# Second recurrence of a two-layer block: rows of C by DMA instead of a TensorE spread and a ScalarE copy, and two banks for the rows of B

## What is computed

```python
def step(state, inp):                       # 256 channels, 16 states
    dt_t, u_t, b_t, c_t, g_t = inp
    a = a_base[None] * (0.5 + g_t)[..., None]
    decay = jnp.exp(dt_t[..., None] * a)
    state = decay * state + dt_t[..., None] * b_t[:, None, :] * u_t[..., None]
    y_t = jnp.sum(state * c_t[:, None, :], axis=-1) + D_param * u_t
    return (state, y_t)
```

## Time and profile before

| | us |
|---|---|
| median of three runs | 652.9 |
| lowest, highest | 650.82, 654.76 |
| span of the profiled execution | 652.0 |
| busy in it: TensorE, VectorE, ScalarE, GpSimd | 565.3, 529.9, 391.0, 394.1 |
| recurrence of layer 1, first to last scan | 266.7 to 494.2 |

### The profile page before, as it was taken

How to read it: one execution, slowest core, us unless ns; L and a number is a source line. 1 busy time by engine, 2 the same in 40 slices (tenths; PEclk the granted TensorE clock), 3 DMA queues, 4 the chain that set the end, 5 groups by cost and what they waited for, 6 DMA issues and landing times.

```text
span 652.0 us, 6791 instructions
## 1 busy us (share of the span) xinstructions
PE 565.3 (87%) x1896; PEld 318.0 (49%) x1896; DVE 529.9 (81%) x729; ACT 391.0 (60%) x670; POOL 394.1 (60%) x345
## 2 busy tenths in 40 slices
PE   6698668899999877898887869768789999999997
PEld 3233222376778522333332323323345778888885
DVE  1979997656779678899999999999998857666674
ACT  5675333687123498878867655766664575555553
POOL 0035896661000202499999999999875547566665
PEclk9898877999799998799999898999989999999999
DMA  8100000800210001000000000001003333434430
GB/s 309 39 2 1 0 1 1 343 1 1 66 66 1 1 0 48 2 0 1 2 24 25 25 25 25 24 14 50 0 0 115 98 114 125 127 106 147 110 102 18
DMA packets 14598, 35.13 MB, mean 54 GB/s; under 512 B 1952, under 2 KB 2240, under 8 KB 13952
## 3 DMA queue, kind: packets, MB, share of 16 engines
q1 hardware_dynamic: 14560, 34.69, 16.6%
HBM read 33.48 MB, written 1.20 MB: 53 GB/s over the span
## 4 chain that ended last, share of the span: by engine, by line
PE 33%; DVE 29%; issue 15%; POOL 13%; ACT 9%; DMA 1%; POOLq 0%; DVEq 0%; SPq 0%; ACTq 0%
DVE arena L1932 12%; POOL h_parts L2147 9%; PE ps L1081 7%; DVE arena L1907 5%; PE ps L1016 3%; PE ps L687 3%; DVE arena L1660 3%; POOL arena L2012 3%; PE ps L866 2%; DVE ps L1644 2%; DVE ps L1853 1%; PE ps L883 1%; PE ps L944 1%; PE ps L801 1%; PE ps L804 1%
## 5 line engine op out<-in xcount | busy, mean ns | idle before, releaser
L2012 POOL TENSOR_TENSOR arena<-arena 128x512 f32<-128x512 f32 x184 | 226.4, 1265 | 22.8 <-DVE arena L1932 16.8
L1932 DVE TENSOR_TENSOR_SCAN arena<-ps,carry,arena 128x512 f32<-128x512 f32 x128 | 156.8, 1268 | 0.0
L1016 PE MATMUL ps<-arena,core 128*128 128x512 f32 x256 | 128.2, 623 | 0.9 <-POOL arena L2012 0.7
L1487 ACT ACTIVATE ps<-arena,abase 128x512 f32<-128x512 f32 x128 | 88.0, 692 | 63.6 <-DVE arena L1932 62.8
L2147 POOL TENSOR_TENSOR h_parts<-arena,h_parts 128x512 fp32r<-128x512 f32 x68 | 87.7, 1290 | 63.3 <-ACT h_parts L1527 62.3
L1081 PE MATMUL ps<-x_parts,w_hi 128*128 128x512 f32 x272 | 100.4, 408 | 0.4 <-DVE arena L2005 0.4
L1907 DVE TENSOR_TENSOR arena<-ps,arena 128x1024 f32<-128x1024 f32 x64 | 77.1, 1205 | 4.6 <-PE ps L1119 4.5
L2000 DVE TENSOR_TENSOR ps<-ps,arena 128x512 f32<-128x512 f32 x64 | 44.6, 697 | 44.1 <-PE ps L1081 35.9
L1119 PE MATMUL ps<-bc,sel 96*128 96x512 bf16 x128 | 44.5, 394 | 37.9 <-ACT arena L1476 23.4
L1535 ACT ACTIVATE arena<-ps 128x512 f32<-128x512 f32 x68 | 40.6, 598 | 61.2 <-PE ps L1081 60.1
L1016 PEld LDWEIGHTS ps<-arena,core 128*128 128x128 f32 x256 | 50.2, 198 | 41.6 <-issue 26.0
(11 more groups left out here) (258 smaller groups left out, 1002.9 us busy)
## 6 DMA issues: line engine op xcount, KB each, us to landing
arena<-weight_rows SPq DMA_DIRECT2D x64, 256.0 KB, 3.3
arena<-in_wB SPq DMA_DIRECT2D x2, 2048.0 KB, 12.5
arena<-in_wD SPq DMA_DIRECT2D x8, 384.0 KB, 3.2
arena<-in_cstB SPq DMA_DIRECT2D x1, 1368.0 KB, 5.9
wC<-in_wC SPq DMA_DIRECT2D x1, 1056.0 KB, 11.8
x<-in_x SPq DMA_DIRECT2D x4, 256.0 KB, 4.8
arena<-slot_rows SPq DMA_DIRECT2D x4, 256.0 KB, 3.7
arena<-scale_rows SPq DMA_DIRECT2D x4, 256.0 KB, 3.6
```

What stands on the lines that cost most here:

```text
L1016: mm(bank(c + 2 * (i % 2)), CORE_("eye"), PRC[:, (2 * q + c) % PR_RING, :], start=False, stop=(n == NS - 1)).then_inc(*done(f"y{n}_{c}", i))
L1487: A(bank(6 + c), ch(DTG[:, c, :], i), ACT.Exp, scale=ABASE[:, c * NS + n:c * NS + n + 1]).then_inc(*done(f"dec{n}_{c}", i))
L1932: nc.vector.tensor_tensor_scan(ST[:, k % ST_RING, :], bank(6 + c), DBU[:, (2 * q + c) % DBU_RING, :], CARRY[:, k:k + 1], ALU.mult, ALU.add ...
L2012: mul = lambda o, a, b: nc.gpsimd.tensor_tensor(o, a, b, ALU.mult)
```

## The change

The rows of C no longer pass TensorE, bank 5 and ScalarE. `bc_hi` is made with a scale that is 1 for rows of B and 0 for rows of C (a new column `b_rows` of the constants), so R1 holds the rows of C whole, in f32. SP stores these 16 rows of a chunk in DRAM, and loads one row per turn over all partitions into the same ring `CBR`. GpSimd waits for the load instead of the copy. Bank 5 becomes a second bank for the rows of B. The raw expert weights, from the third part on, are issued among the rows of C at set turns (`RAW_AT`). The selection matrix loses its half for C, and a constant that nothing used (`EYEB`) goes.

```diff
+RAW_AT = {24 + 4 * k: k + 2 for k in range(WD_PARTS - 2)}
...
-            act += [(f"c_copy{n}", i)] + decs if q else decs + [("c_copy0", 0)]
+            act += decs
...
-            pe += [(f"b{n}", i), (f"c{n}", i)]
+            pe.append((f"b{n}", i))
...
+            def keep_c_rows(i):
+
+                sp.wait_ge(*upto("bc_r1", i))
+                sp.dma_start(c_rows[i * NS:(i + 1) * NS, :], ch(R1, i)[NS:2 * NS]).then_inc(c_rows_kept, 16)
+
+            def c_row(q):
+
+                i = q // NS
+                if q % NS == 0:
+                    sp.wait_ge(c_rows_kept, 16 * (i + 1))
+                if q >= C_RING:
+                    sp.wait_ge(*turn("sc{}_1", q - C_RING))
+                sp.dma_start(CBR[:, q % C_RING, :], c_rows[q:q + 1, :].partition_broadcast(P)).then_inc(c_loaded[q % C_RING], 16)
...
+            keep_c_rows(0)
+            for q in range(C_RING):
+                c_row(q)
+            for i in range(1, NCH):
+                keep_c_rows(i)
+            sp.wait_ge(*upto(f"conv1_{KC - 2}", NCH - 1))
+            raw_weights(0)
+            raw_weights(1)
+            for q in range(C_RING, NQ):
+                c_row(q)
+                if q in RAW_AT:
+                    raw_weights(RAW_AT[q])
...
-                if m == 0:
-                    pe.wait_ge(*upto(f"dbu{NS - 1}", NCH - 1))
-                elif m == 1:
-                    pe.wait_ge(*upto(f"c_copy{NS - 1}", NCH - 1))
+                if m < 2:
+                    pe.wait_ge(*turn("dbu{}", NQ - 2 + m))
...
-                for kind, b, last_use, row in ("b", 4, "dbu{}", n), ("c", 5, "c_copy{}", NS + n):
-                    if q:
-                        pe.wait_ge(*turn(last_use, q - 1))
-                    mm(bank(b), sel[:, row, :], BC[:, i * N:(i + 1) * N], start=True, stop=True).then_inc(*done(f"{kind}{n}", i))
+                if q >= 2:
+                    pe.wait_ge(*turn("dbu{}", q - 2))
+                mm(bank(4 + q % 2), sel[:, n, :], BC[:, i * N:(i + 1) * N], start=True, stop=True).then_inc(*done(f"b{n}", i))
...
-                A(ch(BC, i), half(1, i, BC3), ACT.Copy).then_inc(*done("bc_hi", i))
+                A(ch(BC, i), half(1, i, BC3), ACT.Copy, scale=col("b_rows")[0:BC3]).then_inc(*done("bc_hi", i))
...
-            nc.vector.tensor_copy(ch(BC, LAST), half(1, LAST, BC3)).then_inc(*done("bc_hi", LAST))
+            ts(ch(BC, LAST), half(1, LAST, BC3), col("b_rows")[0:BC3], None, ALU.mult).then_inc(*done("bc_hi", LAST))
...
-                    pool.wait_ge(*upto(f"c_copy{n}", i))
+                    pool.wait_ge(c_loaded[q % C_RING], 16 * (q // C_RING + 1))
```

More of the change, by code:

```diff
@@ L104 @@
 VEC = ["ln1_w", "mu_r", "mu_k", "mu_v", "mu_w", "mu_g", "w0", "u", "gn_w", "gn_b", "ln2_w",
-       "c0", "c1", "eps5", "eps6", "two", "one", "x_low", "x_sign", "w_low", "w_sign",
+       "c0", "c1", "b_rows", "eps5", "eps6", "two", "one", "x_low", "x_sign", "w_low", "w_sign",
        "dt_b0", "dt_b1", "D0", "D1", "cb0", "cb1"] + [f"cw{c}_{j}" for c in range(DI) for j in range(KC)] + \
@@ L364, with build @@
 G_LAST = ["g_half"]
[L367 removed]
+def build(nc, X_in, vec_in, core_in, cst_in, wA_in, wmod_in, cstB_in, wB1_in, wB2_in, wC_in, sel_in, wD_in, out):
     f32 = mybir.dt.float32
@@ L399, in build @@
         slots_loaded, scales_loaded = ([sem(f"{name}_loaded{i}") for i in range(NCH)] for name in ("slots", "scales"))
+        c_rows = nc.dram_tensor("c_rows", (NQ, N), f32, kind="Internal").ap()
+        c_rows_kept = sem("c_rows_kept")
+        c_loaded = [sem(f"c_loaded{k}") for k in range(C_RING)]
         row_loaded = [sem(f"row_loaded{k}") for k in range(W_SLOTS)]
@@ L645, in _, with raw_weights @@
                     sp.dma_start(ch(dst, i), token_rows[k][i:i + 1, :].partition_broadcast(P)).then_inc(landed[i], 16)
-            sp.wait_ge(*upto(f"conv1_{KC - 2}", NCH - 1))
-            for k in range(WD_PARTS):
+            def keep_c_rows(i):
[8 more added lines that the diff above has]
+                sp.dma_start(CBR[:, q % C_RING, :], c_rows[q:q + 1, :].partition_broadcast(P)).then_inc(c_loaded[q % C_RING], 16)
+            def raw_weights(k):
                 if k >= 2:
@@ L1470, in decays @@
                 i, n = divmod(q, NS)
-                def c_copy():
-                    act.wait_ge(*upto(f"c{n}", i))
-                    if q >= C_RING:
-                        act.wait_ge(*turn("sc{}_1", q - C_RING))
-                    A(CBR[:, q % C_RING, :], bank(5), ACT.Copy).then_inc(*done(f"c_copy{n}", i))
-                if q:
-                    c_copy()
-                else:
+                if q == 0:
                     act.wait_ge(*upto("sp_1", LAST))
```

24 lines of the change are left out of this document (10 added, 14 removed).

## The result

| | before | after |
|---|---|---|
| median of 20 runs each, us | 653.92 | 651.43 |
| lowest, highest | 650.82, 655.05 | 650.31, 653.31 |
| span of the profiled execution | 652.0 | 649.8 |

The ratio of the two kernels is 0.9974, with a 95% interval of 0.9962 to 0.9985 (the medians alone give 0.9962, the means 0.9972). The change gains 0.26% here, half of what the prediction called measurable, where 0.6% was forecast. The same kernel was run twice more beside the experiments, and stood there at 0.9988 and 0.9992, with intervals that take in 1. By the three ratios the gain is 0.5 to 1.7 us, not 4.

What follows compares the result with a forecast made beforehand. VectorE was taken as the bound, 3.49 us a turn. Span 652.0 - 4.7 at the seam (gaps -2.07, start +0.1 included) + 0.7 for the clock = 648.0; the median, 0.9 above the span, made it 648.9 us, range 646.3 to 650.3.

Steps and rivals of the forecast that it cites:

- (1): TensorE in the recurrence: 64 matmuls spreading C go, 25 us of TensorE beside VectorE's turns, not on the path.
- (2): ScalarE in the recurrence: 64 copies out of bank 5 go, 37.3 us, by itself worth nothing; TensorE's wait goes.
- (3): Recurrence: a second bank gives rows of B a turn more, removing VectorE's gaps of 0.31, 0.96 and 0.80: -2.07 us.
- (4): Start of the recurrence: the 2.41 us gap stays nearly whole, scaled copies cost more; net +0.1 us, bounds -0.2 and +0.4.
- (5): Seam from recurrence to experts: second up product starts at 492.2, not 496.9, so -4.7 us, containing the 2.07.
- 0.7 for the clock: Seam: a low TensorE clock takes back 0.7 us of the gain, bounds nothing and 2.6 us.
- (6): SP's queue: four stores and 64 loads for rows of C, 3.3 us each, hidden by GpSimd's work: cost nothing.
- (7): GpSimd in the recurrence: little slack, 0.3 us left at turn 35; DMA slowdown taken as 0, up to +1.1 us.
- the 2.6 of the clock: Seam: upper bound of what a low TensorE clock takes back, all the seam gives beyond the gaps.
- the first: Rival at the seam: TensorE stays at the low clock, only the gaps are gained; gain 2, 650.9 us, chance 0.18.
- Slower: Rival in the recurrence: TensorE at the low clock for many turns becomes the bound; +8, 656.9 us, chance 0.13.

Runs made afterwards that it cites:

- Experiment 1: Changed kernel with TensorE issuing the row of B of turn q+1 ahead of the y sum of turn q-4: 649.5 us, 0.9939 of the kernel before.
- experiment 3: Changed kernel with a single bank for the rows of B instead of two: 1.0009 and, second time, 0.9989 of the kernel before.
- experiment 8: Changed kernel with GpSimd's nine w_lo splits replaced by plain copies on ScalarE: 651.48 us, 0.9967 of the kernel before.
- experiment 9: Changed kernel with a TensorE wait for ScalarE's decay put back behind each row of B: median 652.59 us, 1.0017 of the kernel before.
- experiment 6: Changed kernel without the 60 loads of rows of C from turn 4 on: 652.67 us, 0.9988 of the kernel before.
- experiment 5: Changed kernel run again word for word, twice: 652.18 us and 652.45 us, 0.9988 and 0.9992 of the kernel before.

## Why the prediction was wrong, step by step

- **(1), (2) matmuls and copies of C.** Right: 64 of each gone, and worth nothing by themselves.
- **(3) two banks, -2.07 us.** This step failed. It set the gaps against the turn that the second bank adds, and then took from the trace of before that "Late next is the y sum of turn q-4 ... it was ready in time at all three". But there TensorE's matmuls stood 23.4 us at the spread rows until ScalarE had copied, and this had covered GpSimd's lag: they waited 0.7 us for GpSimd at the y sums. With the waits for the copy gone TensorE comes to most y sums ahead of GpSimd, its matmuls stand there 23.1 us (its weight loads 60.8, where they stood 8.9), and where it comes out at the low clock the row behind it is late: from 383.14 the sum (3.78), D·u (1.91) and the row (0.53) take until 388.96, 5.8 us against a turn of 3.49. The recurrence shortened by 0.46 to 0.60 us, not 2.07. Experiment 1 shows that with the row ahead of the sum the 2.07 come, experiment 3 that the second bank without that order brings nothing, and experiment 8 points to GpSimd's lag as what the order passes on.
- **(4) the start, +0.1.** The start wait stayed (2.19 us against 2.41) and the scaled copies took 0.68 us, both as said. The start was longer by 0.06, 0.33 and 0.51 us in three profiles: right in sign, twice within the bounds of -0.2 and +0.4 and once above.
- **(5) the seam.** Right in mechanism, with less room than it had reckoned. The second up product stands at 494.20, not 496.9, and VectorE's idle time behind the last scan fell by 2.1 us in each of three profiles, where 2.7 less 0.7 for the clock were forecast beyond the gaps. The three y sums and the gate products do end before bank 6 is free, but only by 0.31 us: the last sum starts at 490.84, not at 487.8 to 489.5, as TensorE's timeline of the kernel after has it:

```profile
490.84 1.88 PE L1045 MATMUL ps<-arena,core 128*128 128x512 f32 x4
493.03 0.50 PE L1110 MATMUL ps<-x_parts,w_hi 128*128 128x512 f32 x1 [0.31 <-DVE arena L1948]
...
494.20 0.50 PE L1110 MATMUL ps<-x_parts,w_hi 128*128 128x512 f32 x1 [0.21 <-DVE arena L1948]
```

  That the wait for the copy was what had made the seam late is borne out by experiments 3 and 9: one bank and no wait for a copy leave 1.28 and 1.30 us, two banks with a wait for ScalarE 2.88 in the one execution profiled. One thing was missing: the next limit. The first expert product on VectorE now waits for ScalarE, which loads its activation table and makes the first silu after the last decay:

```profile
492.97 1.28 ACT L1536 ACT_TABLE_LOAD   x1
494.27 1.09 ACT L1551 ACTIVATE arena<-ps 128x512 f32<-128x512 f32 x2
```

- **(6), (7) the DMAs.** Right: 3.1 us per load, no wait of GpSimd for one, and its pace unchanged (experiment 6). GpSimd's slack at turn 35 never came to matter, since no scan waited for a carry. (The 56 products that the prediction counted up to turn 35 should be 72, two for each of 36 turns, and its bound for a slower GpSimd 1.8 us less the slack. The term was taken as 0, and GpSimd's pace did not change.)
- **The sum and its range.** The steps as worded allow a smaller gain than the range that was drawn from them: 4.7 at the seam less the 2.6 of the clock and the 0.3 of a worse start are 1.8 us, or 651.1, not 2.6 and 650.3. The measured 651.43 lies outside even so, and the step that failed is (3).
- **The rivals.** What happened is the mirror of the first: the seam gave its part and the gaps nothing. "Slower", with TensorE at the low clock for many turns, was wrong in size: the clock did fall to 0.76 in the stretch from 380 to 400 us, but that is (1 - 0.76) / 0.5 x 20 = 9.6 us at the low clock, under three turns, and not the thirty in a row that the rival needs. It was right that a pause, the low clock behind it and a late row belong together.

**What stays open.** The parts of the three profiles of the change, measured against the one profile of the kernel before (start, recurrence, seam and the 155 us behind it), add up to 2.4 to 2.6 us gained, while the runs give 0.5 to 1.7; for the new order they add up to 6.7 us, and the runs give 4.0. Part of this lies ahead of the parts compared, in stages whose steps no edit touches: VectorE's last `layer_in` starts at 235.65 us in the profile before, at 236.02, 235.27 and 237.60 in the three of the change, and at 238.34 with the new order. What moves it stays open. The one profiled execution before, at 652.0 us, need not be typical: its runs lie between 650.4 and 655.1 us. Why the granted clock falls in one turn of an execution and in another of the next was not settled, nor why it is full behind 440 us in both executions with one bank and in none of the change.

## What to carry to other kernels

A second buffer helps only as far as the engine that fills it can come early: look at what stands ahead of the filling step in its engine's order, and at what that waits for. When a wait is taken away, ask which later wait it had covered; that a later step "was ready in time" in the old trace may only mean that the engine which takes it came late. An order and a buffer can each be worth nothing or less alone and 0.6% together, as here, so try them together. And compare waits of one kind only: those of TensorE's weight loads went from 8.9 to 60.8 us at the y sum, those of its matmuls from 0.7 to 23.1.

## What was not expected of the hardware

- The same program has its stalls at different turns in different executions (389.00 and 403.46; 343.27 and 402.84; 345.76 and 405.39 us), with sums within 0.15 us, as the granted clock falls in different places (experiment 5). A forecast that takes away the gaps of one profile by name takes away a sample.
- Two small things came as the prediction had them, and are now measured in this kernel itself. A ScalarE copy of 96 x 512 from PSUM to bf16 takes 0.68 us with a scale read from memory (at 242.08 us in the kernel after), 0.59 without one. And 60 row loads of 256 KB beside GpSimd's products left these at 1282 ns, against 1283 without them.
